# Experts' token rows loaded in 32x32 blocks and turned by VectorE instead of TensorE

## The reference

```python
logits = xn @ router_w                       # 8 experts
topv, topi = jax.lax.top_k(softmax(logits), 2)
for e in range(E):                           # E = 8, D = 256, F = 1024
    out = out + comb[:, e:e + 1] * _swiglu(xn, gate_up_w[e], down_w[e])
out = out + _swiglu(xn, shared_gate_up_w, shared_down_w)
# _swiglu: gate, up = split(x @ gu); silu(clip(gate, -10, 10)) * up @ dn
```

## Time and profile before

| | us |
|---|---|
| median of 3 executions | 1184.25 (1182.82 to 1186.65) |
| the profiled execution: time | 1177.22 |
| the profiled execution: span of its instructions | 1175.1 |
| of it: first matmul of the group loop starts at | 470.16 |
| PE busy | 1079.8 (92%) |
| DVE busy | 834.3 (71%) |
| ACT busy | 655.0 (56%) |
| POOL busy | 299.7 (26%) |

### The profile page before, as it was taken

One profiled execution on the slowest core, in us unless ns is written; L12 is line 12 of the kernel. 1 busy time (PEld: TensorE's weight loads), 2 busy tenths in 40 slices (PEclk: granted clock), 3 DMA queues, 4 the chain that ended last, 5 costly groups with the idle time before them and its releaser, 6 DMA issues.

```text
span 1175.1 us, 24151 instructions
## 1 busy us (share of the span) xinstructions
PE 1079.8 (92%) x7492; PEld 958.3 (82%) x7492; DVE 834.3 (71%) x2113; ACT 655.0 (56%) x1325; POOL 299.7 (26%) x358
## 2 busy tenths in 40 slices
PE   4889999899979997999999999999999999999940
PEld 2666776677757664999999999999999999999940
DVE  5996899898878765666666666666666666666645
ACT  6778867778674363444544454544445544554425
POOL 1142032733441534012211221122122212211225
PEclk9999999999999999999999999999999999999975
DMA  8664766974664788523322236746932267211239
GB/s 291 219 216 169 253 227 214 316 242 147 222 230 150 261 287 312 177 56 70 72 54 36 36 84 211 224 131 188 375 74 36 49 219 250 36 21 33 36 90 214
DMA packets 122219, 191.72 MB, mean 163 GB/s; under 512 B 9792, under 2 KB 76864, under 8 KB 122176
## 3 DMA queue, kind: packets, MB, share of 16 engines
q1 hardware_dynamic: 105760, 170.38, 42.6%
q0 software_dynamic: 16416, 20.85, 10.7%
HBM read 295.62 MB, written 86.41 MB: 325 GB/s over the span
## 4 chain that ended last, share of the span: by engine, by line
PE 79%; DVE 8%; issue 3%; DMA 3%; ACT 2%; POOL 2%; SPq 1%; another core or an unknown queue 1%; DVEq 0%; ACTq 0%; POOLq 0%
PE bank L469 13%; PE bank L1354 12%; PE bank L1356 12%; PE bank L1355 12%; PE bank L1365 6%; PE bank L1367 6%; PE bank L1366 6%; PE bank L463 4%; PE bank L464 3%; PE bank L465 3%; PE bank L1342 1%; DMA w_both<-w_split 1%; DVE a_cum L874 1%; DVE xr L1496 1%
## 5 line engine op out<-in xcount | busy, mean ns | idle before, releaser
L1304 POOL DMA_INDIRECT acc_scratch<-cv,ids x78 | 121.1, 1553 | 550.0 <-DVE cv L1444 509.9
L1465 DVE TENSOR_SCALAR cv<-bank 128x256 f32<-128x256 f32 x312 | 132.2, 424 | 181.9 <-PE bank L1356 164.2
L1354 PE MATMUL bank<-h_hi,w_both 128*128 128x256 f32 x936 | 259.9, 278 | 1.5 <-DMA w_both<-w_split 1.5
L1356 PE MATMUL bank<-h_hi,w_both 128*128 128x256 f32 x936 | 258.9, 277 | 0.0
L1355 PE MATMUL bank<-h_hi,w_both 128*128 128x256 f32 x936 | 258.9, 277 | 0.0
L1415 ACT ACTIVATE cv<-cv 128x256 f32<-128x256 f32 x312 | 130.4, 418 | 219.5 <-DVE cv L1465 219.5
L1407 ACT ACTIVATE h_lo<-cv 128x256 fp32r<-128x256 f32 x312 | 129.9, 416 | 114.9 <-DVE cv L1472 112.9
L1354 PEld LDWEIGHTS bank<-h_hi,w_both 128*128 128x128 f32 x936 | 176.2, 188 | 2.1 <-DVE cv L1472 1.9
L1355 PEld LDWEIGHTS bank<-h_hi,w_both 128*128 128x128 f32 x936 | 176.1, 188 | 0.1
L1356 PEld LDWEIGHTS bank<-h_hi,w_both 128*128 128x128 f32 x936 | 175.9, 188 | 0.0
L1472 DVE TENSOR_TENSOR cv<-bank,cv 128x256 f32<-128x256 f32 x312 | 132.5, 425 | 47.7 <-ACT cv L1415 43.3
(11 more groups left out here) (227 smaller groups left out, 2385.7 us busy)
## 6 DMA issues: line engine op xcount, KB each, us to landing
w_both<-w_split SPq DMA_DIRECT2D x228, 512.0 KB
w_both<-w_split SPq DMA_DIRECT2D x228, 256.0 KB
e_raw<-w_e SPq DMA_DIRECT2D x64, 384.0 KB
w_split<-e_high SPq DMA_DIRECT2D x64, 384.0 KB
w_split<-e_raw SPq DMA_DIRECT2D x64, 384.0 KB
xs_hi<-w_split SPq DMA_DIRECT2D x38, 512.0 KB
xs_lo<-w_split SPq DMA_DIRECT2D x38, 512.0 KB
u<-xs_scratch SPq DMA_DIRECT2D x40, 260.0 KB, 3.2
```

Of the source, the lines that this page charges most:

```text
L1354: nc.tensor.matmul(out, gu_hi[f][:, cols], xg_hi[:, par, c, :], start=c == 0, stop=False)
L1356: i = nc.tensor.matmul(out, gu_lo[f][:, cols], xg_hi[:, par, c, :], start=False, stop=c == DC - 1)
L1465: nc.vector.tensor_scalar(gate[:, f % 4, :], gu_ps[f % 2][:, 0:G], CLIP, -CLIP, ALU.min, ALU.max).then_inc(clipped, 1)
```

## The change

Four things are changed together.

1. The rows of a group are no longer loaded by one DMA but by nine. Eight of them move a block column each: 32 of the 256 row values, of all 256 rows, to 32 partitions, so that each 32x32 block lies in SBUF as VectorE's transpose wants it. The ninth (`load_meta`) moves the four extra values of each row to a home of its own.
2. In SyncE's loop the eight go out in pairs, right behind the weights of places 0, 1, 2 and 3, and the ninth behind the weights of place 4. The row's address is read at place 0. The first groups' rows (`rw/3`, and group 2 in `others`) are issued as nine DMAs in a row.
3. TensorE's transposes are gone. VectorE turns the rows of group g + 1 with one 128x256 transpose at place 1 and one at place 4, each between `h_low` and the multiplication with silu. The first of them waits until all nine DMAs have landed. ScalarE reads the turned rows from SBUF and not from PSUM.
4. In the first phase the transposes of group 0 leave TensorE's order, and `turn0/3 turn1/3` and `x0/3 x1/3` stand later in VectorE's, `x0/3 x1/3` later in ScalarE's order.

```diff
-X_AT, D_AT, R_AT = 48, 48, 0
+X_AT, D_AT = 48, 48
+BLK = 32
...
# TensorE's, ScalarE's, VectorE's order (all for batch 3)
-... y1/4 d0.11/3 x0/3 g1/6 d1.7/3 x1/3 d1.8/3 y0/5 ...
+... y1/4 d0.11/3 g1/6 d1.7/3 d1.8/3 y0/5 ...
-... w14/3 x0/3 d1.7/3 w15/3 d1.8/3 s0/6 e0/5 x1/3 s1/6 d1.10/3 e1/5 s0/7 ...
+... w14/3 d1.7/3 w15/3 d1.8/3 s0/6 e0/5 s1/6 d1.10/3 x0/3 e1/5 x1/3 s0/7 ...
-... x0/3 w14/3 ... d1.10/3 x1/3 times1/6 d1.11/3 clip0/7 d1.12/3 clip1/7 times0/7 ...
+... w14/3 ... d1.10/3 turn0/3 turn1/3 times1/6 d1.11/3 clip0/7 d1.12/3 x0/3 clip1/7 x1/3 times0/7 ...
...
     def sync(sp):
+        def load_blocks(row, par):
+            for n in range(LOADS - 1):
+                load_block(row, par, n)
+            load_meta(row, par)
+
+        def load_block(row, par, n):
+            q, at = n // DC, n % DC * P + n // DC * BLK
+            sp.dma_start(rows[q * BLK:(q + 1) * BLK, par, n % DC, :, :],
+                         xs_dram[bass.ds(row, G), at:at + BLK].rearrange("(t i) j -> i t j", i=BLK)).then_inc(rows_loaded[par], 16)
+
+        def load_meta(row, par):
+            sp.dma_start(meta[:, par, :, :], xs_dram[bass.ds(row, G), D:ROW].rearrange("(t p) k -> p t k", p=P)
                          ).then_inc(rows_loaded[par], 16)
...
             for f in range(FC):
                 load_chunk(g, f, e, new)
-                if f == 1:
-                    if not (isinstance(g, int) and g == 0):
-                        sp.wait_ge(x_turned, g * DC + DC)
-                        sp.wait_ge(meta_ready, g)
-                    load_rows(g + 1, 1 - par)
+                if f == 0:
+                    sp.wait_ge(x_turned, g * DC)
+                    row = row_of(g + 1)
+                if f < QUADS:
+                    load_block(row, 1 - par, 2 * f)
+                    load_block(row, 1 - par, 2 * f + 1)
+                if f == QUADS:
+                    sp.wait_ge(meta_ready, g)
+                    load_meta(row, 1 - par)
...
     def tensor(pe):
-                if f == 1:
-                    for c in range(DC):
-                        turn_rows(g + 1, 1 - par, c)
...
     def vector(dve):
+        def turn_rows(g, par, c):
+            if c == 0:
+                dve.wait_ge(rows_loaded[par], g_half(g, par) * (16 * LOADS) + 16 * LOADS)
+            if not (isinstance(g, int) and g == 0):
+                dve.wait_ge(x_f_ready, g * DC + c)
+            nc.vector.transpose(turned[:, c, :], rows[:, par, c, :, :].rearrange("p t j -> p (t j)")).then_inc(x_turned, 1)
...
                     h_low(g - 1, FC - 1)
+                if f in (1, 4):
+                    turn_rows(g + 1, 1 - par, (f - 1) // 3)
                 dve.wait_ge(silu_ready, g * FC + f + 1)
```

More of the change, by code:

```diff
@@ L187, in free @@
         def free(engine, what):
-            if what == "x_ps":
-                engine.wait_ge(yn_ready, 2 * B + 1)
-            elif what == "gu_ps":
+            if what == "gu_ps":
                 engine.wait_ge(s_hid, 4 * B)
@@ L1048, in fullest @@
                 i.then_inc(star_ready, 1)
-            run("vector", {"x": first_lo, "star": fullest, "m": x_moments, "p": split_low, "k": bias_sum, "c": conv_sides, "r": xs_remainder, "dt": delta_unit, "da": da_unit,
+            run("vector", {"x": first_lo, "turn": first_turn, "star": fullest, "m": x_moments, "p": split_low, "k": bias_sum, "c": conv_sides, "r": xs_remainder, "dt": delta_unit, "da": da_unit,
                            "ac": acum_unit, "bx": bx_unit, "h": h_unit, "d": d_stage, "w": w_stage,
@@ L1187, in experts @@
     LAG = 3
-    w_gu, w_d, rows, xg_hi, xg_lo, xg_f, gate, hg_hi, hg_lo, y, acc, x1, small = homes
+    w_gu, w_d, rows, meta, turned, xg_hi, xg_lo, xg_f, gate, hg_hi, hg_lo, y, acc, x1, small = homes
     gu_hi, gu_lo = [part[:, 0:4 * P] for part in w_gu], [part[:, 4 * P:8 * P] for part in w_gu]
@@ L1205, in experts @@
     gu_ps, down_ps = banks[0:2], [banks[2:4], banks[4:6]]
-    x_ps = [banks[6][:, c * G:(c + 1) * G] for c in range(DC)]
     loaded = [sem(f"chunk_loaded{f}") for f in range(FC)]
     rows_loaded = [sem(f"x_rows_loaded{i}") for i in range(2)]
+    QUADS = P // BLK
+    LOADS = DC * QUADS + 1
     x_turned, x_hi_ready, x_f_ready, x_lo_ready = sem("x_turned"), sem("x_hi_ready"), sem("x_f_ready"), sem("x_lo_ready")
@@ L1333, in tensor @@
     def tensor(pe):
-        def turn_rows(g, par, c):
-            if c == 0:
-                pe.wait_ge(rows_loaded[par], (g_half(g, par)) * 16 + 16)
-                if isinstance(g, int) and g == 0:
-                    free(pe, "x_ps")
-            pe.wait_ge(x_f_ready, c + 1 if isinstance(g, int) and g == 0 else g * DC + 1)
-            for t in range(GT):
-                i = nc.tensor.transpose(x_ps[c][:, t * P:(t + 1) * P], rows[:, par, t, c * P:(c + 1) * P], ident[:, :])
-            i.then_inc(x_turned, 1)
         def gate_up(g, par, f):
@@ L1379, in turn @@
                     down(g - 1, 1 - par, FC + f - LAG)
-        def first_turn(b, c):
-            turn_rows(0, 0, c)
         def rest():
@@ L1447, in weigh @@
         def weigh(g, par):
[L1448 to L1449 removed]
+            column = lambda at: meta[:, par, :, at - D:at - D + 1].rearrange("p t k -> p (t k)")
+            dve.wait_ge(rows_loaded[par], g_half(g, par) * (16 * LOADS) + 16 * LOADS)
             if not (isinstance(g, int) and g < 2):
                 dve.wait_ge(y_added[par], g_half(g, par) * 16 * GT)
[L1452 to L1454 removed]
+            nc.vector.scalar_tensor_tensor(out=part[:, :], in0=column(CODE), scalar=group_code[:, bass.ds(g, 1)],
+                                           in1=column(MORE), op0=ALU.is_equal, op1=ALU.mult).then_inc(meta_steps, 1)
+            nc.vector.tensor_copy(ids[:, par, :], column(ID).bitcast(I32))
             dve.wait_ge(meta_steps, g + 1)
[L1456 removed]
+            nc.vector.tensor_tensor(share[:, par, :], part[:, :], column(SECOND), ALU.add).then_inc(meta_ready, 1)
         def h_low(g, f):
@@ L1483, in seeds, with first_turn @@
             dve.sem_inc(y_ready, 2)
+        def first_turn(b, c):
+            turn_rows(0, 0, c)
         def first_lo(b, c):
@@ L1517, in rest @@
             add_x1(NC - 1)
-        return seeds, first_lo, rest
+        return seeds, first_turn, first_lo, rest
     return sync, gpsimd, tensor, scalar, vector
```

41 lines of the change are left out of this document (18 added, 23 removed), and 6 rows, old and new, of the table ORDER.

## The result

The changed kernel takes 1230.13 us (median of 4 runs, 1226.08 to 1232.43); the kernel before took 1183.57 beside it. The ratio is 1.0398, 95% interval [1.0363, 1.0433]: 47 us slower. On a second chip it was 1.0395 [1.0368, 1.0423]. The forecast was 1197 us, range 1175 to 1214. The direction was right; of the loss of 46.6 us the forecast had 13.

What follows compares the result with a forecast made beforehand. TensorE was taken to bound the loop of 39 groups. -19.4 + 20.5 + 7.9 + 4 = +13.0 us gave 1190.2 on the profiled execution; adding the 7.0 by which the runs' median lay higher, 1197 us, range 1175 to 1214.

Steps and rivals of the forecast that it cites:

- What goes: TensorE's loop: the transposes of groups 1 to 39 leave, 0.50 us a group, -19.4 us.
- VectorE and SyncE in a quiet group: Groups without expert change: VectorE's two transposes and SyncE's block issues of 0.55 us fit the spare time, 0 us.
- SyncE becomes the bound: Rival: block issues over about 0.75 us make SyncE lag in quiet groups; about 1220 us, 1248 at worst; chance 0.14.
- The new wait: Expert changes: VectorE waits for the ninth DMA behind later weights, delaying `gate_up(3)` 4.1 us; five single changes +20.5.
- the pair: Two expert-change groups following each other: SyncE falls behind, stalls 4.1 + 5.3 less 1.5 us, +7.9.
- I take 1.0, nearer the bytes: 951.7: Expert change: small packets add 1.0 us to the ninth DMA's landing at 950.7 by bytes; far end 4.7.
- a DMA behind it lands 2.9 later: Expert change, working by issue: place 4's chunk is out at 948.8, so the ninth DMA lands at 951.8.
- The later chunks land while TensorE stands still, so their lateness isn't added: Expert change: late weight chunks fall inside TensorE's wait for VectorE and add nothing to the 4.1 us.
- The first phase: Before the loop: `rw/3` grows from two DMAs to 18, next issue 9.1 us later; +4 us, ends 0 and 9.
- Of these 6.5 us TensorE's shared-expert products hide some 2.5: First phase: the last weights piece, landing near 446, delays ScalarE's rounding; 2.5 of 6.5 us hidden, leaving +4.

Runs made afterwards that it cites:

- eight DMAs of 1-KB packets: Version with rows loaded a whole group earlier, but each of its eight DMAs brings 16 partitions' rows whole in 1-KB packets: 1192.25 us, ratio 1.0164.
- rows a group earlier: Changed kernel, but the blocks for the group after the next are loaded next to the weights of places 4 to 7: 1205.99 us, ratio 1.0212.
- no reload: Changed kernel with all expert-change flags zero, so every group uses the first expert's weights: 1158.03 us, ratio 0.9891.
- GpSimd's stores of zeros: Version with GpSimd issuing all row loads, but GpSimd also issues the 8 stores of zero rows ahead of the loop: 1168.35 us, ratio 0.9978.
- two DMAs of small packets: Changed kernel's one-DMA variant, but the rows come in two DMAs of 128 rows, each cut into 1024 runs of 128 bytes: 1182.23 us, ratio 1.0084.
- first rows moved: Changed kernel, but the first phase issues group 0's rows behind the shared expert's fourth store, group 1's behind the weights' last store: 1228.5 us, ratio 1.0395.
- rows on GpSimd: Against the changed kernel, GpSimd issues all row and column loads, 4 DMAs of 256-byte runs a group, for the third group ahead: 1169.68 us, ratio 0.9989.
- one-DMA version: Changed kernel, but a group's row values come in one DMA in the old layout, the extra values in a second, behind place 1's weights: 1156.4 us, ratio 0.9869.

## Why the prediction was wrong

By its own steps, in the profiled executions:

- *What goes*: forecast -19.4, measured -17.3, 38 intervals of 0.455 and not 39 of 0.50. Right.
- *VectorE and SyncE in a quiet group*: 0, right. The transposition takes 0.436 us (median of 80), a block's issue about 0.55 with its address (2 in 0.88 and the gap behind them), as taken. A block's issue of over 0.75, the condition of *SyncE becomes the bound*, is so excluded.
- *The new wait*: its mechanism was right, its size wasn't. TensorE's last wait is 3.6 to 3.9 us where 4.1 stood, and that is luck. What counts is how late `gate_up(3)` starts, since it also holds what TensorE waited for weights before: 6.1 to 6.5 us in six changes and 4.8 in the second of the pair, 43.0 in all, where 5 x 4.1 and 9.4 for the pair, 29.9, stood.
- The step that failed here: "I take 1.0, nearer the bytes: 951.7" and, in the other working, "a DMA behind it lands 2.9 later". SyncE's issues were right: place 4 starts 12.3 us after place 0 (973.36 to 985.65) where 12.1 stood. But the ninth DMA lands 4.3 to 5.5 us behind its issue and not 2.9, as the rows' DMA of the earlier trace rows did in a change. Against the bytes alone (950.7, so 8.2 us into the group) VectorE goes on 3.3 to 3.7 us later in six changes; the sum had 1.0 there, for the small packets, with 4.7 as the far end. The DMA engines were full at 296 to 316 GB/s where I had reckoned with 399. The Trainium skill's page DMA: Bandwidth & Descriptors (section Queues, rings and completion order) has a DMA engine consume a queue's descriptors in ring order. The trace agrees: the weights of place 4 landed at 992.39 and the last of the nine at 992.62.
- "The later chunks land while TensorE stands still, so their lateness isn't added" held: TensorE waits 11.4 us for the chunks of places 1 and 2, but VectorE's wait ends later, so these are inside the 43.0. They do bound what another order of VectorE's work can win: with VectorE turning at places 3 and 4 TensorE's waits for weights were 13.8.
- Not in the sum at all, the second step that failed: the clock. The earlier trace rows show PEclk 1.00 in the loop, and I read that as a property of the loop and not of its never standing still. Half clock behind the stalls cost 15.2 us in the 7 changes. 43.0 + 15.2 = 58.2 of the 59.1; the rest isn't assigned.
- *The first phase*: forecast +4, measured +10. SyncE's part was right: the first rows' issues take 8.8 us longer where 9.1 stood; 1.9 more was there before the first of them (426.64 against 424.75). The step that failed is "Of these 6.5 us TensorE's shared-expert products hide some 2.5", and ahead of it that the last piece's load would land at 446, 3 us behind its issue. It was issued at 443.93 and ScalarE went on at 448.94, 5.0 later; so ScalarE came 9.5 later than before, and nothing was hidden.

The forecast missed the span by 35.9 us: 27.9 in the changes (13.1 for the late `gate_up(3)`, 15.2 for the clock, 0.9 unassigned, less 1.3, since the changes of before lost 2.8 and not the 1.5 that stood there), 6.0 in the first phase and 2.1 in what goes. The range's upper end, 1214, was set by stalls and issue costs. It had no case in which one stall sets off another loss, and without the clock's 15.2 us the kernel would have come out at 1215, still at its end.

## What to carry to other kernels

A wait put in front of an engine's other work costs the bound engine its length and then what the bound engine loses by having stood still; in this kernel 43 us and then 15. When a queue's issuer gets more to do, compare its time with the bound engine's for the worst group, not the usual one: here 16.4 us against over 18, in 7 of 39 groups. Count small packets in the same way where the DMA engines are full: each of the two sufficed to lengthen a change by 4 us, and 27 of 59 us were left once VectorE's order was changed. Moving when the waiting instruction stands (one or two places later) was worth 35 us and is the first thing to try; loading earlier on the same queue won less, 22 us by the ratios.

## What the runs showed of the hardware

- The granted clock fell to 0.50 at every stall of TensorE of 2.9 to 5.8 us in the loop, with DMA engines full or idle, for 3.4 or 6.8 us; the fall came between 3.3 us before TensorE went on and 1.5 us after. It stayed at 1.00 at the waits of 0.8 to 1.8 us. In between the runs have both: it fell at 1.88 and 2.07 us (eight DMAs of 1-KB packets), 1.94 (rows a group earlier), 2.14 (no reload), 2.29 (GpSimd's stores of zeros) and 2.60 (two DMAs of small packets), and stayed at 1.88 (first rows moved), 1.89 and 2.43 (two DMAs of small packets) and 2.11 and 2.25 (rows on GpSimd). So there the length of a wait alone doesn't decide it. The case of 2.07:
```profile
738.80:742.20 3.40, 1.33 (x12) 1.13 (x11) 1.37 (x4) 1.14 (x3) 0.00 (x0) 0.99 1.07 319
742.20:745.60 3.40, 3.40 (x17) 3.40 (x18) 0.61 (x2) 0.15 (x1) 0.00 (x0) 0.50 1.02 359
```
- An issue on SyncE isn't of fixed price: 0.37 to 0.46 us for the 4-KB load of the one-DMA version and the changed kernel, and 2.6 to 4.2 behind 2048 packets of 128 bytes and two chunks of weights.
- Full DMA engines moved less in the changed kernel's expert changes: some 300 GB/s (median of the 3-us stretches in which they were full), against some 390 in the kernel before and in the one-DMA version, and 350 with eight DMAs of 1-KB packets. So the packets of 128 bytes are a part of it, but not shown to be all.
- VectorE's transposition of a 128x256 tile of 4-byte elements in 32x32 blocks takes 0.436 us (median of 80), about what its other operations on such a tile take (0.41).
